# A mixture-of-experts stage with its down projection turned round and its combine weights spread by DMA

## The chip, the cores and the metric

One Trainium2 chip, one NeuronCore. The metric is the device time of one execution of the whole program in microseconds (us), lower is better. The core's engines run side by side, each through its own instruction list, and meet only at semaphores: TensorE (PE, with its weight loads as PEld), VectorE (DVE), ScalarE (ACT), GpSimd (POOL) and SyncE (SP), which here issues every DMA. A DMA moves data by up to 16 DMA engines.

## What is computed

A stack of four layers on 2 x 512 tokens of width 256: cross attention, a gated feed-forward, and so on. The change lies in one stage, the feed-forward of the second layer (`L1_ffn`), a mixture of 64 routed experts of hidden width 64, of which each token keeps 8, and 2 shared experts of hidden width 512:

```python
gates = softmax(x @ router_w + router_b)         # [T, 64]; the 8 largest are kept, divided by their sum
for e in range(64):                              # routed experts
    y += cw[:, e] * (silu(x @ w1[e] + b1[e]) @ w2[e] + b2[e])
for s in range(2):                               # shared experts, weight 1
    y += silu(x @ sw1[s] + sb1[s]) @ sw2[s] + sb2[s]
out = x_residual + y
```

(x is the normalised input; this is a shortening of the reference in plain words.) The kernel computes all 64 experts for all 1024 tokens; an expert that a token did not keep has combine weight `cw` 0.

## The kernel before

The program is a row of stages, each ended by a barrier of all engines. The stage here is `l1_experts_phase`. Its work is cut into N = 40 units of 128 hidden columns: 8 units of the shared experts (n = 0 to 7), then 32 units that each hold two routed experts (64 + 64 columns). T is 1024 tokens, P is 128, KC = 2 is the number of 128-chunks of the width 256, and Q = 2 halves of 512 tokens are called q.

The engines are software pipelined by hand. In period n, written by each engine's `period` function:

- TensorE computes the up projection of unit n into PSUM tile `up` (for each half q, six matmuls of 512 moving columns: weights `up_hi`/`up_lo` stationary, tokens `xnT_hi`/`xnT_lo` moving), for a routed unit one more matmul per half into `weight`, and then the down projection of unit n - 1 into PSUM tile `out`.
- ScalarE applies silu to `up` (L1617), splits the next unit's up weights into a high part (L1606, L1607), rounds `hidden` to its high part `h_hi` (L1625) and splits `dn_raw` (L1635).
- VectorE multiplies silu by the combine weights (L1682, `hidden`) and forms the low part `h_lo` (L1686). GpSimd forms the low parts of the weights (L1651, L1664).
- SyncE loads unit n's weights in two transfers, `load_up` (L1534, 128 partitions of 1028 bytes) and `load_dn` (L1537, 128 partitions of 1 KB), into raw buffers that there are two of (s = n % 2).

Every fp32 product is three matmuls of split operands, in `mm3` (L73 to L75): high by high, then the two mixed ones. In the down projection each matmul has 128 tokens of `h` stationary and 256 columns of `dn` moving, 8 token chunks by 3 matmuls = 24 per unit.

**The combine weights.** `l1_router` makes them as `exps` [128 tokens, 8 chunks, 64 experts] on VectorE during shared periods 0 to 3. A routed unit needs them with hidden columns on the partitions: partition j of unit n wants the 1024 weights of the expert that column j belongs to. Before, they are split into three bf16 parts (`split_parts`, after period 4), turned by TensorE (`turn_parts`, after period 5), copied by ScalarE, and then each period's matmul with the 0/1 matrix `select` (L1571) writes each expert's row to 64 partitions of PSUM tile `weight`. A second turn (`turn_weights`, after period 6) makes `cwT` [64 experts, 1024 tokens] in fp32, with which `add_biases` (after period 7) adds the b2 terms.

At the end, in period 40, the last down projection ends bank by bank, and VectorE adds `out` to the residual `g.x` and takes statistics (L1692, L139). The next stage is `l2_project_phase`.

Two transfers of an earlier stage come into the prediction. `return_inverses` (L838) stores a 128-partition tile of 16 values per partition into `inverse_rows`, which has 4 partitions: 128 rows of 64 bytes. `load_max` (L620) stores `neg_rows`, 12 partitions of 512 bytes, into 3 partitions of `q_stack`. A third, `phi_a<-fside` (L1838), loads 128 rows of 4 KB into 128 partitions. `sums<-avs` (L832) writes 32 partitions.

Of the kernel before, what the change touches and what calls it, by code (L numbers as in the profile page):

```python
# [17 lines left out]
F32 = mybir.dt.float32  # L18
F32R = mybir.dt.float32r
BF16 = mybir.dt.bfloat16  # L20
# [1340 lines left out]
def l1_router(nc, ctx, g, d, banks):  # L1361
# [4 lines left out]
    HALF = E1 // 2  # L1366

# [7 lines left out]
    parts = sb("cw_parts", [P, TC, 2, 3, HALF], BF16)  # L1375
    r = Shared()
    r.cwT = sb("cwT", [P, T])
    r.cw_partsT = sb("cw_partsT", [3 * HALF, 2, T], BF16)
# [3 lines left out]
    parts_done, parts_turned, dve_steps = g.sem("cw_parts_done"), g.sem("cw_parts_turned"), g.sem("r1_dve_steps")  # L1382
    r.parts_copied, cw_turned, r.cw_copied = g.sem("cw_parts_copied"), g.sem("cw_turned_done"), g.sem("cw_copied")
# [15 lines left out]
    def turn_parts(pe):  # L1399
        pe.wait_ge(parts_done, 1)  # L1400
        pe.wait_ge(ready, 1)
        for h in range(2):
            for c in range(TC):
                last = pe.transpose(banks.bitcast(BF16)[0:3 * HALF, h, c * P:(c + 1) * P],
                                    parts[:, c, h, :, :].rearrange("p a e -> p (a e)"), g.ident16[:, :])
            last.then_inc(parts_turned, 1)
# [12 lines left out]
    def copy_parts(act):  # L1419
        for h in range(2):  # L1420
            act.wait_ge(parts_turned, h + 1)
            act.activation(r.cw_partsT[:, h, :], banks.bitcast(BF16)[0:3 * HALF, h, :], ACT.Copy).then_inc(r.parts_copied, 1)

    def copy_weights(act):
        act.wait_ge(cw_turned, 1)
        act.activation(r.cwT[0:E1, :], banks[0:E1, :, :], ACT.Copy).then_inc(r.cw_copied, 1)
# [22 lines left out]
    def keep_largest(dve):  # L1449
# [4 lines left out]
        divide(dve)  # L1454

    def split_parts(dve):
        halves = exps[:, :, :].rearrange("p c (h e) -> p c h e", h=2)
        rest = shifted[:, :, :].rearrange("p c (h e) -> p c h e", h=2)
        own.link(dve.tensor_copy(parts[:, :, :, 0, :], halves))
        own.link(dve.tensor_tensor(rest, halves, parts[:, :, :, 0, :], ALU.subtract))  # L1460
# [995 lines left out]
```

## Time and profile before

| what | value |
|---|---|
| median of 3 runs | 1619.1 us (1615.59 to 1621.07) |
| profiled execution, span from its first to its last instruction | 1613.2 us |
| what lies around the span (median less span) | 5.9 us |
| the stage here, from its first DMA issue to the next stage's | 883.4 to 1151.5 us of the span |
| mean granted TensorE clock | 0.952 of full |
| TensorE busy over the span | 93% |

The page of the profile has no time of its own for the profiled execution beside its span, so the span and the 5.9 us are what the sums are made against. Times inside the span are counted from its first instruction. A matmul's recorded duration is longer than the distance to the next one, since matmuls are pipelined; what a stream of them costs is read from start to start.

### The profile page before, as it was taken

Reading aid. Unit: us, or ns where it says so; the run is one execution under the profiler, and the core shown is the slowest. Engines: PE = TensorE matmul, PEld = TensorE weight load, DVE = VectorE, ACT = ScalarE, POOL = GpSimd, SP = SyncE. Lnnn points to the kernel's source line nnn. Section 1 sums busy time; section 2 is a strip of 40 time slices with the busy share of each in tenths; the row PEclk is TensorE's granted clock in tenths of the full one; section 3 lists DMA queues with packets and bytes.
Section 4 is the critical chain, followed back from the end, with each engine's and each line's share of the span. In section 5 each row is a group of like instructions: output and inputs, shape, how many; then the busy total and the mean of one; then the engine's idle time right before and its main releaser. Section 6 shows DMA issues by size and latency. Waiting matters only on the chain. (4 is left out here: it accounts for less than half of the span.)

```text
span 1613.2 us, 26635 instructions
## 1 busy us (share of the span) xinstructions
PE 1503.4 (93%) x9326; PEld 1222.4 (76%) x9326; DVE 923.3 (57%) x1698; ACT 705.9 (44%) x1102; POOL 286.0 (18%) x317
## 2 busy tenths in 40 slices
PE   5899999899999999999996999999789799998894
PEld 4444444688888888888886888888677688887884
DVE  6788886545455554555558534444556445556555
ACT  5266666244343443434332555555333434343431
POOL 2111100022122221212210222222010112220110
PEclk8899999799999999999998899999899899999996
DMA  6711210111111111111100111111011211101000
GB/s 232 221 31 32 60 30 3 53 40 39 59 39 59 39 50 47 39 59 39 59 7 29 47 40 39 46 39 46 23 53 52 73 39 39 59 26 40 0 0 27
DMA packets 44836, 78.78 MB, mean 49 GB/s; under 512 B 7567, under 2 KB 27541, under 8 KB 43893
## 3 DMA queue, kind: packets, MB, share of 16 engines
q1 hardware_dynamic: 44789, 78.14, 15.8%
q8 instruction: 31, 0.51, 0.1%
q14 instruction: 16, 0.13, 0.0%
HBM read 67.40 MB, written 10.49 MB: 48 GB/s over the span
## 5 line engine op out<-in xcount | busy, mean ns | idle before, releaser
L1238 DVE TENSOR_TENSOR hidden_l<-silu_l,up_l 128x512 f32<-128x512 f32 x176 | 121.0, 688 | 305.7 <-ACT silu_l L1178 305.7
L73 PE MATMUL out_l<-dn_hi_l,h_hi_l 128*128 128x256 f32 x1024 | 295.4, 288 | 0.7 <-POOL dn_lo_l L1664 0.7
L1178 ACT ACTIVATE silu_l<-gate_l 128x512 f32<-128x512 f32 x176 | 105.2, 598 | 425.2 <-PE up_l L75 425.2
L75 PE MATMUL out_l<-dn_hi_l,h_lo_l 128*128 128x256 f32 x1024 | 289.5, 283 | 0.0
L74 PE MATMUL out_l<-dn_lo_l,h_hi_l 128*128 128x256 f32 x1024 | 289.4, 283 | 0.0
L73 PEld LDWEIGHTS out_l<-dn_hi_l,h_hi_l 128*128 128x128 f32 x1024 | 196.4, 192 | 2.8 <-issue 0.8
L74 PEld LDWEIGHTS out_l<-dn_lo_l,h_hi_l 128*128 128x128 f32 x1024 | 196.0, 191 | 2.8
L75 PEld LDWEIGHTS out_l<-dn_hi_l,h_lo_l 128*128 128x128 f32 x1024 | 196.0, 191 | 0.0
L798 DVE TENSOR_REDUCE maxima<-a_scores 128x1 f32<-128x512 f32 x256 | 164.6, 685 | 40.3 <-PE a_scores L736 39.1
L1210 POOL TENSOR_TENSOR gu_lo_l<-gu_raw_l,gu_hi_l 128x1024 fp32r<-128x1024 f32 x42 | 100.7, 2398 | 407.7 <-ACT gu_hi_l L1170 407.7
L1262 DVE SCALAR_TENSOR_TENSOR x_sb<-out_l,cw,x_sb 128x256 f32<-128x256 f32 x352 | 150.0, 477 | 30.6 <-PE out_l L75 24.9
L765 ACT ACTIVATE probs<-b_scores 128x1024 f32<-128x1024 f32 x128 | 131.0, 1023 | 66.6 <-PE b_scores L695 64.5
L73 PE MATMUL gate_l<-xnT_hi_n,gu_hi_l 128*128 128x512 f32 x352 | 139.7, 397 | 4.3 <-DVE xnT_lo_n L191 4.3
L1244 DVE TENSOR_TENSOR h_lo_l<-hidden_l,h_hi_l 128x512 fp32r<-128x512 f32 x176 | 139.3, 791 | 4.4
L74 PE MATMUL gate_l<-xnT_lo_n,gu_hi_l 128*128 128x512 f32 x352 | 139.3, 396 | 0.0
L75 PE MATMUL gate_l<-xnT_hi_n,gu_lo_l 128*128 128x512 f32 x352 | 138.9, 395 | 0.0
L73 PE MATMUL up_l<-xnT_hi_n,gu_hi_l 128*128 128x512 f32 x352 | 138.4, 393 | 0.0
L75 PE MATMUL up_l<-xnT_hi_n,gu_lo_l 128*128 128x512 f32 x352 | 138.0, 392 | 0.0
L74 PE MATMUL up_l<-xnT_lo_n,gu_hi_l 128*128 128x512 f32 x352 | 138.0, 392 | 0.0
L1183 ACT ACTIVATE h_hi_l<-hidden_l 128x512 fp32r<-128x512 f32 x176 | 110.3, 627 | 10.3 <-DVE hidden_l L1238 10.3
L1682 DVE TENSOR_TENSOR hidden_l<-silu_l,weight_l 128x512 f32<-128x512 f32 x64 | 44.0, 687 | 111.7 <-ACT silu_l L1617 111.7
L1617 ACT ACTIVATE silu_l<-up_l,b_l 128x512 f32<-128x512 f32 x80 | 55.1, 689 | 108.1 <-PE weight_l L1571 88.9
(369 smaller groups left out, 2835.4 us busy)
## 6 DMA issues: line engine op xcount, KB each, us to landing
gu_raw_l<-w_units SPq DMA_DIRECT2D x44, 512.0 KB, 3.8
dn_raw_l<-w_units SPq DMA_DIRECT2D x44, 256.0 KB, 2.7
k_stack<-k_stacks SPq DMA_DIRECT2D x8, 768.0 KB, 5.7
up_raw_l<-w SPq DMA_DIRECT2D x40, 128.5 KB, 2.1
dn_raw_l<-w SPq DMA_DIRECT2D x40, 128.0 KB, 2.1
phi_a<-fside SPq DMA_DIRECT2D x8, 512.0 KB, 3.3
k_stacks<-kq_parts SPq DMA_DIRECT2D x8, 384.0 KB, 2.6
q_stack<-q_stacks SPq DMA_DIRECT2D x8, 384.0 KB, 6.4
```

The costliest lines, as they stand in the source:

```text
L73: pe.matmul(out, lhs[0], rhs[0], start=start, stop=False, skip_group_check=True)
L74: pe.matmul(out, lhs[0], rhs[1], start=False, stop=False, skip_group_check=True)
L75: return pe.matmul(out, lhs[1], rhs[0], start=False, stop=stop, skip_group_check=True)
L765: act.activation(probs[u % 4][:, :, :], b_scores[:, u % 2, :, :], ACT.Exp, scale=SCALE).then_inc(exp_done, 1)
L798: dve.tensor_reduce(maxima[k // 16][:, i // 2, i % 2:i % 2 + 1], a_scores[:, k % 2, :], X, ALU.max).then_inc(a_read, 1)
L1178: act.activation(silu[:, q % 2, :], gate[:, q % 2, :], ACT.Silu).then_inc(silu_done, 1)
L1183: act.activation(h_hi[s][:, fc, half * 512:(half + 1) * 512], hidden[:, q % 2, :], ACT.Copy).then_inc(h_hi_done, 1)
L1210: pool.tensor_tensor(gu_lo[s][:, :, :, :], gu_raw[s][:, :, :, :], f32(gu_hi[s][:, :, :, :]), ALU.subtract).then_inc(gu_lo_done, 1)
L1238: dve.tensor_tensor(hidden[:, q % 2, :], silu[:, q % 2, :], up[:, q % 2, :], ALU.mult).then_inc(hidden_done, 1)
L1244: dve.tensor_tensor(h_lo[s][:, fc, t], hidden[:, q % 2, :], f32(h_hi[s][:, fc, t]), ALU.subtract).then_inc(h_lo_done, 1)
L1262: last = dve.scalar_tensor_tensor(g.x[:, c, :], out[:, b, j, :], weight, g.x[:, c, :], ALU.mult, ALU.add)
L1617: act.activation(silu[:, q, :], up[:, q, :], ACT.Silu, bias=b1[s][:, :]).then_inc(silu_done, 1)
```

## The change

1. **Down projection turned round.** The down weights become stationary and 512 tokens move: for each half of the tokens and each 128-chunk of the width one `mm3`, 4 x 3 = 12 matmuls of 512 columns per unit. `out` now holds the transposed output. `add_biases` is turned likewise. At the end ScalarE copies `out` to the new SBUF tile `outT`, TensorE turns it back in 16 transposes into the PSUM tile `front` (which `up` is now a part of), and VectorE adds that to the residual.
2. **Combine weights spread by DMA.** The matrix `select`, its matmul in each routed period, and the split, turn and copy of bf16 parts are gone. `turn_weights` runs after period 5 rather than 6. `cwT` is stored to DRAM as `cw_rows` [64, 1024]; for each routed unit `load_spread` reads its two rows of 4 KB, each 64 times over, into the 128 partitions of `spread[s]` (two buffers). VectorE waits for it before the unit's multiplications. The experts of a unit are now 2m and 2m + 1.

```diff
@@ l1_router @@
     def turn_weights(pe):
+        pe.wait_ge(kept, 1)
         for c in range(TC):
-            if c % 4 == 0:
-                pe.wait_ge(r.parts_copied, c // 4 + 1)
             last = pe.transpose(banks[0:E1, c // 4, c % 4 * P:(c % 4 + 1) * P], exps[:, c, :], g.ident[:, :])
...
@@ block.sync @@
-                sp.dma_start(select[:, :, :], d["select"]).then_inc(b2_loaded, 16)
-                with sp.Fori(0, (N - 2) // 2) as i:
+                def load_spread(m, pair, s):
+
+                    rows = g.cw_rows[bass.ds(2 * pair, 2), :].rearrange("e (o t) -> e o t", o=1).to_broadcast([2, H1, T])
+                    sp.dma_start(spread[s][:, :], rows).then_inc(spread_loaded[s], 16)
+
+                def load_unit(m, s):
+
+                    sp.wait_ge(up_lo_done, m - 1)
+                    load_up(m, s)
+                    sp.wait_ge(dn_lo_done, m - 1)
+                    load_dn(m, s)
+
+                for m in range(2, NS):
+                    load_unit(m, m % 2)
+                sp.wait_ge(router.cw_copied, 1)
+                sp.dma_start(g.cw_rows[:, :], router.cwT[0:E1, :]).then_inc(rows_stored, 16)
+                sp.wait_ge(rows_stored, 16)
+                for m in (NS, NS + 1):
+                    load_spread(m, m - NS, m % 2)
+                    load_unit(m, m % 2)
+                with sp.Fori(0, (N - NS - 2) // 2) as i:
                     for s in range(2):
-                        sp.wait_ge(up_lo_done, 2 * i + s + 1)
-                        load_up(2 * i + s + 2, s)
-                        sp.wait_ge(dn_lo_done, 2 * i + s + 1)
-                        load_dn(2 * i + s + 2, s)
+                        m = NS + 2 + 2 * i + s
+                        load_unit(m, s)
+                        sp.wait_ge(hidden_done, Q * (m - 1))
+                        load_spread(m, 2 + 2 * i + s, s)
@@ block.tensor, period @@
-                            if pair is not None:
-                                pe.wait_ge(hidden_done, Q * n + q - 1)
-                                last = pe.matmul(weight[:, q, :], select[:, bass.ds(pair, 1), :].rearrange("p o m -> p (o m)"),
-                                                 router.cw_partsT[:, s, t], start=True, stop=True)
...
-                        for c in range(TC):
-                            t = slice(c * P, (c + 1) * P)
-                            last = mm3(pe, out[:, c // 2, c % 2, :], (h_hi[o][:, t], h_lo[o][:, t]),
-                                       (dn_hi[o][:, :], dn_lo[o][:, :]), isinstance(n, int) and n == 1 and c % 2 == 0, not has_up)
+                        for h in range(2):
+                            t = slice(h * 512, (h + 1) * 512)
+                            for dc in range(KC):
+                                f = slice(dc * P, (dc + 1) * P)
+                                last = mm3(pe, out[:, h, dc, :], (dn_hi[o][:, f], dn_lo[o][:, f]),
+                                           (h_hi[o][:, t], h_lo[o][:, t]), isinstance(n, int) and n == 1, not has_up)
...
+                def return_output(pe):
+
+                    for h in range(2):
+                        pe.wait_ge(outT_done, KC * (h + 1))
+                        for c in range(4):
+                            for dc in range(KC):
+                                last = pe.transpose(front[:, 2 * h + c // 2, c % 2 * D + dc * P:c % 2 * D + (dc + 1) * P],
+                                                    outT[:, h, dc, c * P:(c + 1) * P], g.ident[:, :])
+                            if c % 2 == 1:
+                                last.then_inc(returned, 1)
@@ block.scalar @@
+                def copy_output(act):
+                    for h in range(2):
+                        for dc in range(KC):
+                            act.wait_ge(bank_done, KC * h + dc + 1)
+                            act.activation(outT[:, h, dc, :], out[:, h, dc, :], ACT.Copy).then_inc(outT_done, 1)
@@ block.vector, period @@
+                        dve.wait_ge(spread_loaded[s], 16 * (uses - NS // 2))
...
-                            dve.tensor_tensor(hidden[:, q, :], silu[:, q, :], weight[:, q, :], ALU.mult).then_inc(hidden_done, 1)
+                            dve.tensor_tensor(hidden[:, q, :], silu[:, q, :], spread[s][:, q * 512:(q + 1) * 512], ALU.mult).then_inc(hidden_done, 1)
@@ four_layers @@
+        g.cw_rows = nc.dram_tensor("cw_rows", [E1, T], F32, kind="Internal").ap()
```

**Where instructions move.** First SyncE's queue in the experts' stage. Before, the loop over the units holds two loads per unit:

```order
L1546 ISA
L1534 ISA
L1534 DMA up_raw_l<-w 128x257
L1537 ISA
L1537 DMA dn_raw_l<-w 128x256
L1534 ISA
```

(ISA rows are waits and register work.) In the changed program, at the same place, the store of `cw_rows` and the first spread stand ahead of unit 8's loads:

```order
L1516 DMA dn_raw_l<-w 128x256
L1540 DMA cw_rows<-cwT 64x1024
L1528 DMA spread_l<-cw_rows 128x1x1024
L1513 DMA up_raw_l<-w 128x257
L1516 DMA dn_raw_l<-w 128x256
L1528 DMA spread_l<-cw_rows 128x1x1024
```

So unit 8's up weights are now queued behind a store, a wait for its landing, and a spread; and in the loop that follows, each unit's two loads are followed by its spread on the same queue.

Second, TensorE's queue in a routed period. Before, from the end of the up projection's second half into the down projection:

```order
L75 MATMUL up_l<-xnT_hi_n,up_lo_l 128x512
L1571 MATMUL weight_l<-cw_partsT,select_l 128x512
L73 MATMUL out_l<-dn_hi_l,h_hi_l 128x256
L74 MATMUL out_l<-dn_lo_l,h_hi_l 128x256
L75 MATMUL out_l<-dn_hi_l,h_lo_l 128x256
```

and the same place of the changed program:

```order
L75 MATMUL front_l<-xnT_hi_n,up_lo_l 128x512
L73 MATMUL out_l<-h_hi_l,dn_hi_l 128x512
L74 MATMUL out_l<-h_lo_l,dn_hi_l 128x512
L75 MATMUL out_l<-h_hi_l,dn_lo_l 128x512
```

The matmul with `select` has gone, and the three-matmul group of 256 columns, which stood 8 times, is one of 512 columns, which stands 4 times.

## Rows read from the trace of the kernel before

**Rows 1.** The page, part 1: busy time and share of the span by engine.

```profile
PE 1503.4 (93%) x9326; PEld 1222.4 (76%) x9326; DVE 923.3 (57%) x1698; ACT 705.9 (44%) x1102; POOL 286.0 (18%) x317
```

**Rows 2.** Busy time by stretch: shared periods, routed periods; clock, DMA share, GB/s last.

```profile
core 0: us, PE busy (x) PEld busy (x) DVE busy (x) ACT busy (x) POOL busy (x), PEclk, DMA share, GB/s
...
889.43:946.21 56.78, 56.52 (x353) 51.09 (x353) 23.03 (x56) 32.69 (x65) 13.62 (x16) 0.94 0.15 39
946.21:1143.25 197.04, 196.41 (x1218) 165.43 (x1217) 85.42 (x128) 103.00 (x222) 51.57 (x63) 1.00 0.15 39
```

**Rows 3.** The timeline, TensorE in one routed period: start, duration, instruction.

```profile
1001.55 0.39 PE L73 MATMUL up_l<-xnT_hi_n,up_hi_l 128*128 128x512 f32 x1
...
1002.71 0.39 PE L75 MATMUL up_l<-xnT_hi_n,up_lo_l 128*128 128x512 f32 x1
...
1004.93 0.28 PE L74 MATMUL out_l<-dn_lo_l,h_hi_l 128*128 128x256 f32 x1
...
1007.20 0.28 PE L75 MATMUL out_l<-dn_hi_l,h_lo_l 128*128 128x256 f32 x1
```

**Rows 4.** The select matmul: all 64, with first and last start (us).

```profile
L1571 PE MATMUL weight_l<-cw_partsT,select_l x64: 391/392/392, 947.8 to 1139.4; 96*128 96x512 bf16 x64
```

**Rows 5.** The longest waits in the routed periods: in total, times, longest.

```profile
DVE hidden_l L1682 <- ACT silu_l L1617: 103.2, 61, 2.6
```

**Rows 6.** The timeline from the end of period 5 to the first routed period.

```profile
929.31 1.05 PE L1404 MATMUL weight_l<-ident_sb,cw_parts 128*96 128x128 bf16 x16
...
935.92 1.03 PE L1412 MATMUL weight_l<-ident_sb,exps 128*64 128x128 f32 x8
...
941.72 1.00 ACT L1426 ACTIVATE cwT<-weight_l 64x1024 f32<-64x1024 f32 x1
...
942.87 3.69 PE L1594 MATMUL out_l<-b_l,cwT 66*128 66x256 f32 x16 [0.26 <-ACT cwT L1426]
```

**Rows 7.** DMA issues of the whole trace: count, KB each, median us to landing.

```profile
dn_raw_l<-w SPq DMA_DIRECT2D x40, 128.0 KB, 2.1
phi_a<-fside SPq DMA_DIRECT2D x8, 512.0 KB, 3.3
...
out<-x_sb SPq DMA_DIRECT2D x4, 256.0 KB, 2.0
```

**Rows 8.** DMA from 286 to 288 us, where inverse_rows is written.

```profile
DMA packets 132, 0.01 MB, mean 4 GB/s; under 512 B 132, under 2 KB 132, under 8 KB 132
...
inverse_rows<-sums SPq DMA_DIRECT2D x1, 8.0 KB
```

**Rows 9.** DMA from 259.5 to 261.2 us, where neg_rows goes to q_stack.

```profile
q1 hardware_dynamic: 15, 0.01, 1.3%
...
q_stack<-neg_rows SPq DMA_DIRECT2D x1, 6.0 KB
```

**Rows 10.** DMA from 1200 to 1206 us, one load of phi_a, in 40 slices.

```profile
DMA  0000000000000939358989998300000000000000
GB/s 0 0 0 0 0 0 0 0 0 0 0 0 0 164 82 218 82 246 328 382 328 410 437 410 328 137 0 0 0 0 0 0 0 0 0 0 0 0 0 0
...
q1 hardware_dynamic: 144, 0.52, 26.7%
```

**Rows 11.** That load alone by stretch: us, clock, share of 16 DMA engines, GB/s.

```profile
1202.04:1203.90 1.86, 1.00 0.87 286
```

**Rows 12.** The timeline of the last unit, from its first weighted product on.

```profile
1138.88 0.69 DVE L1682 TENSOR_TENSOR hidden_l<-silu_l,weight_l 128x512 f32<-128x512 f32 x1 [2.40 <-ACT silu_l L1617]
...
1143.28 0.35 PE L73 MATMUL out_l<-dn_hi_l,h_hi_l 128*128 128x256 f32 x1 [0.66 <-POOL dn_lo_l L1664]
...
1149.11 0.75 DVE L139 BATCH_NORM_STATS2 stats_sb<-x_sb 128x6 f32<-128x256 f32 x2
```

**Rows 13.** The timeline, TensorE in the next stage, just after it stood idle.

```profile
1157.89 0.63 PE L75 MATMUL acc_p<-ctxT_hi_sb,wqkv_lo_p 128*128 128x512 f32 x1
...
1158.32 0.63 PE L73 MATMUL acc_p<-ctxT_hi_sb,wqkv_hi_p 128*128 128x512 f32 x1
```

More of the change, by code:

```diff
@@ L1492, in l1_experts_phase @@
         b2 = sb("b2", [E1 + ES1, D])
-        select = sb("select", [3 * E1 // 2, PAIRS1 // 2, P], BF16)
-        up = ctx.enter_context(nc.psum_tensor("up_l1", [P, 2, 512], F32))
-        weight = ctx.enter_context(nc.psum_tensor("weight_l1", [P, 2, 512], F32))
-        out = ctx.enter_context(nc.psum_tensor("out_l1", [P, TC // 2, 2, D], F32))
+        spread = two("spread", [P, T])
+        outT = sb("outT", [P, 2, KC, 512])
+        front = ctx.enter_context(nc.psum_tensor("front_l1", [P, 4, 512], F32))
+        up, routing = front[:, 0:2, :], front[:, 2:4, :]
+        out = ctx.enter_context(nc.psum_tensor("out_l1", [P, 2, KC, 512], F32))
         def sem(name):
@@ L1579, in period @@
                         pe.wait_ge(h_lo_done, Q * n)
-                        for c in range(TC):
-                            t = slice(c * P, (c + 1) * P)
-                            last = mm3(pe, out[:, c // 2, c % 2, :], (h_hi[o][:, t], h_lo[o][:, t]),
-                                       (dn_hi[o][:, :], dn_lo[o][:, :]), isinstance(n, int) and n == 1 and c % 2 == 0, not has_up)
-                            if not has_up and c % 2 == 1:
-                                last.then_inc(bank_done, 1)
+                        for h in range(2):
[4 more added lines that the diff above has]
+                                           (h_hi[o][:, t], h_lo[o][:, t]), isinstance(n, int) and n == 1, not has_up)
+                                if not has_up:
+                                    last.then_inc(bank_done, 1)
                         if has_up:
@@ L1589, in add_biases @@
                 def add_biases(pe):
[L1591 removed]
+                    pe.wait_ge(b2_loaded, 16)
                     pe.wait_ge(router.cw_copied, 1)
[L1593 to L1595 removed]
+                    for h in range(2):
+                        for dc in range(KC):
+                            pe.matmul(out[:, h, dc, :], b2[:, dc * P:(dc + 1) * P], router.cwT[0:E1 + ES1, h * 512:(h + 1) * 512],
+                                      start=False, stop=False, skip_group_check=True)
+                def return_output(pe):
[7 more added lines that the diff above has]
+                                last.then_inc(returned, 1)
                 pe.sem_inc(down_free, 2)
@@ L1599, in _ @@
                 norm.on_tensor(pe)
-                periods(pe, period, {0: router.take_logits, 5: router.turn_parts, 6: router.turn_weights, 7: add_biases})
+                periods(pe, period, {0: router.take_logits, 5: router.turn_weights, 7: add_biases})
+                return_output(pe)
             @block.scalar
@@ L1644, in _ @@
                 norm.high(act, 1)
-                periods(act, period, {1: router.exponentials, 5: router.copy_parts, NS - 1: last_copies})
+                periods(act, period, {1: router.exponentials, 5: router.copy_weights, NS - 1: last_shared})
+                copy_output(act)
             @block.gpsimd
@@ L1672, in _, with period @@
             def _(dve):
-                def period(n, s, uses, next_uses, pair):
+                def period(n, s, uses, next_uses):
                     if uses is None:
@@ L2410, in _arrange @@
         if n >= len(shared):
-            pair, half = divmod(n - len(shared), 2)
-            e = half * (E1 // 2) + 2 * pair
+            e = 2 * (n - len(shared))
             up = np.concatenate([i["L1_ffn_w1"][e], i["L1_ffn_w1"][e + 1]], axis=1)
```

82 lines of the change are left out of this document (29 added, 53 removed).

## The prediction

> **What bounds the kernel now.** I read the page's busy times first: TensorE is busy 93% of the span, no other engine over 57% [rows 1]. Then the windows of this stage: TensorE works 56.5 of 56.8 us in the shared periods and 196.4 of 197.0 us in the routed ones, at full clock there, while the DMA engines are 15% busy [rows 2]. The waits of the routed periods hold no DMA: VectorE waits for ScalarE, which follows TensorE [rows 5]. So here time is TensorE's instruction stream. From start to start, a 512-column matmul costs (1002.71 - 1001.55) / 5 = 0.232 us and a 256-column one (1007.20 - 1004.93) / 19 = 0.1195 us [rows 3]. The period follows from both: 14 x 0.232 + 24 x 0.1195 = 6.12 us, and the select matmuls say the same, 191.6 us from first to last less 1.6 inside a period, over 31 periods = 6.13 us [rows 4].
>
> **The change on TensorE.** A routed period becomes 12 + 12 matmuls of 512 columns: 24 x 0.232 = 5.57 us, 0.56 less. Nearly all of that is the two select matmuls; the turned projection itself gives 24 x 0.1195 - 12 x 0.232 = 0.08 us. The first turn of 16 small transposes (1.05 us, [rows 6]) goes too, the biases stay the same number of columns. If TensorE stayed the bound, this would be worth some 19 us. Whether it does hangs on the new transfer.
>
> **How long a spread takes.** It moves 128 rows of 4 KB, 512 KB, as much as one load of phi_a, which lands in 3.3 us [rows 7]. But the source is written as 2 rows, each read 64 times, and the trace shows that a transfer's outermost count matters. Packets beyond the data rows are completions, one from each DMA engine used: phi_a, 128 rows outermost on both sides, has 144 = 128 + 16 [rows 10]. inverse_rows, 128 rows at the source and 4 outermost at the destination, has 132 = 128 + 4 [rows 8]. neg_rows, 12 at the source and 3 at the destination, has 15 = 12 + 3 [rows 9]. In all three the number of engines is the largest up to 16 that divides both outermost counts. For 2 and 128 that is 2. I take two engines, each with 64 rows of 4 KB.
>
> The Trainium skill has this as a rule, in DMA: Bandwidth & Descriptors, "Why a DMA increments its semaphore by 16 and not by 1": the engines used are the largest number up to 16 that divides both patterns' slowest dimension other than 1, and its rules for kernel authors warn of just such a leading small count. The three rows above agree; by it too the spread has 2 engines, and the sum below is unchanged.
>
> A 4 KB row on one engine: phi_a's best slice is 437 GB/s on 16 engines = 27.3 GB/s each, 0.150 us a row; the mean of its last seven full slices is 375 GB/s, 0.175 us [rows 10]; over the whole load, 286 GB/s on 87% of 16 engines is 20.5 GB/s each, 0.20 us [rows 11], and simply 1.86 us for 8 rows is 0.23, start-up and all. A spread pays the start-up once in 64 rows, and 14 engines do not compete with it, so I take 0.16, near the best slice, and keep 0.150 and 0.23. 64 x 0.16 = 10.2 us. The same two engines also carry 16 of the rows of about 1 KB of each unit's up and down weights: 39 GB/s at a share of 0.15 of 16 engines is 16 GB/s each, 0.06 us a row [rows 2], 1.0 us. **So the two engines are taken for 11.2 us per unit, twice TensorE's 5.57.**
>
> **Does the queue keep them busy?** Two spread buffers are there. Spread m + 2 is issued once VectorE has multiplied unit m and GpSimd has ended its dn_lo, for which I estimate 5 us after spread m has landed, from the tail [rows 12]: first product at 1138.88, last unit's dn_lo released at 1143.28, 4.4. Some 1 us later it reaches the engines. That is well within the 11.2 us that spread m + 1 takes, so the engines run without a gap. VectorE now waits in every routed period; behind it stand h_lo and with it the down projection, and ScalarE's h_hi. The next unit's up weights stand behind the spread on the same two engines, so ScalarE's split and TensorE's up projection start late as well, but they land just behind it and add nothing to the period.
>
> TensorE will stand idle about half of each period, and where it did so before, 512 columns cost 1158.32 - 1157.89 = 0.43 us [rows 13], the lower of its two clocks. Even then 24 x 0.43 = 10.3 us fit into 11.2. I cost that at nothing in the loop; it would be bound only if the spread took under 9.
>
> **The sum.** Positions in the span. Period 5 of TensorE ends at 929.31 [rows 6], less 5 x 0.08: 928.9. The turn of the weights 1.03 and the copy 1.00 [rows 6] give 930.9. The store, 256 KB, is like that of out, 2.0 to landing [rows 7], plus 0.4 to issue: 933.3. A transfer's fixed part is 2.1 for a load of 8 small rows per engine [rows 7] less 8 x 0.06 = 1.6; the first spread lands at 933.3 + 1.6 + 10.2 = 945.1, the second 11.2 later, 956.3. The first weighted product of unit 9 waits for it. Thirty more units at 11.2: 956.3 + 336 = 1292.3 for unit 39. Before, this product began at 1138.88 [rows 12]. **+153.4 us.**
>
> The tail before: 10.98 us from there to the end of the last statistics at 1149.86 [rows 12]. After: the second product no longer waits for its silu, so the down projection starts at +3.5 instead of +4.4; 12 matmuls at 0.43 = 5.1; the last copy 0.7; the last 8 transposes, 1.03 at full clock [rows 6], 1.7 estimated at the lower; add and statistics 1.4: 12.6. **+1.7 us** (with the full clock +0.6).
>
> Total +155.1 us: on the span 1613.2 + 155.1 = 1768.3, and with 5.9 around it, which is on the median 1619.1 + 155.1 = **1774 us**.
>
> **The rivals.**
>
> *The change does what it says (16 engines).* Then a spread lands in about the 3.3 us of phi_a, is issued a period ahead and stays hidden while it lands within some 6.5 us; TensorE remains the bound. 32 x 0.56 + 7 x 0.08 + 1.05 = 19.5 saved, 0.6 lost in the tail: 1600 us. For it: the copies are equal in size to those that keep up now. Against it: rows 8 and 9, both of them transfers whose two sides differ in shape as this one's do. It decides from somewhere between 4 and 8 engines: with 4 a unit takes them 32 x 0.16 + 1.0 = 6.1 us, as much as a period now; with 8, 3.6, under TensorE's 5.57. Chance 0.07. The Trainium skill's fit for a transfer (the same page, "Anatomy of one DMA", 2.0 us + bytes / 436 GB/s) gives 3.2 us for 512 KB and would lead here; it has no term for the number of engines.
>
> *Two engines, dearer rows.* Reading one 4 KB row over and over, or gaps between transfers, could make a row cost phi_a's 0.20 to 0.23 us. Each 0.01 is 0.64 us a unit, on 32 spreads 20 us: 1856 to 1917 us. For it: phi_a over its whole length; against it, that start-up is most of the difference. Chance 0.12.
>
> *TensorE's lower clock decides.* If, at 0.43 us a matmul, up and down projection also had to wait on one another's results, TensorE's 10.3 us plus about 1.8 for splitting late weights would make 12.1 a period: 0.9 x 30 = 27 on top, 1801 us. Against it: those 1.8 us overlap the down projection of the unit before. Chance 0.08, inside my range.
>
> *The forecast itself*, two engines at 0.150 to 0.175 us a row: 0.73.
>
> **How the numbers follow.** At 0.150 a row the sum falls by 0.64 x 32 = 20 us, and if the small rows cost 0.05, by 5 more: 1749; at 0.175 it rises by 31: 1805. The range takes these, the clock rival, and a little of the dearer rows: 1747 to 1835 us, which leaves out the 16-engine case and most of the dearer one. About 0.3% (5 us) is what a measurement of this kernel can tell from no change. Faster by more: 0.07 (the first rival). Within it: 0.01, since only about 4 engines would land there. Slower: 0.92.
>
> **What would show it.** Right: of each spread, 128 packets and 2 completions; 11 us from product to product of successive units; VectorE waiting for spread_l in some 31 periods, 5 us each or more; DMA share near 2/16 of the engines plus the weights' part, at some 70 GB/s; a granted clock below 1 in the routed periods. Step by step on TensorE: 0.232 us from one turned down matmul to the next wherever the clock is full. Wrong: if the spread lands in under 6 us, the change is a gain of some 19 us and my whole sum falls; if periods are 11 us but VectorE waits for ScalarE, the late weights decide and not the spread.

## The result and the profile after

| | before | changed |
|---|---|---|
| median, range, runs | 1617.7 us (1615.6 to 1621.1, 4) | 1777.9 us (1777.4 to 1778.4, 4) |
| span of the profiled execution | 1613.2 us | 1776.4 us |
| mean granted clock | 0.952 | 0.914 |

The ratio is 1.098 (95% interval 1.0965 to 1.1002): the changed kernel is 160 us slower. The forecast was 1774 us, the range 1747 to 1835.

The page of the changed kernel: part 1; then from part 5 the group of the weighted products with the idle time before it; then from part 6 the transfers (KB each, us to landing).

```profile
PE 1553.1 (87%) x8774; PEld 1237.4 (70%) x8774; DVE 922.5 (52%) x1694; ACT 706.6 (40%) x1104; POOL 286.1 (16%) x317
...
L1699 DVE TENSOR_TENSOR hidden_l<-silu_l,spread_l 128x512 f32<-128x512 f32 x64 | 45.8, 717 | 258.3 <-DMA spread_l<-cw_rows 230.6
...
spread_l<-cw_rows SPq DMA_DIRECT2D x32, 512.0 KB
...
up_raw_l<-w SPq DMA_DIRECT2D x40, 128.5 KB, 16.3
dn_raw_l<-w SPq DMA_DIRECT2D x40, 128.0 KB, 7.4
```

VectorE stood 230.6 us before its 64 products for the spread, where no wait on a DMA was before [rows 5]. The down weights, 2.1 us to landing in [rows 7], now take 7.4, and the up weights, issued behind a spread, 16.3: two of the engines that carry them have a spread to move as well. (In e7 below, with no spread in the loop, both land in 2.1 us.) The page gives no landing for the spreads; it is read from the product that waits.

The windows over the routed periods, as [rows 2]: us, busy time and count of each engine, clock, DMA share, GB/s.

```profile
core 0: us, PE busy (x) PEld busy (x) DVE busy (x) ACT busy (x) POOL busy (x), PEclk, DMA share, GB/s
950.00:1300.00 350.00, 238.52 (x768) 181.31 (x768) 86.82 (x128) 104.00 (x226) 52.24 (x64) 0.80 0.20 69
```

768 matmuls, 24 for each of 32 units, take TensorE 238.5 of 350 us even at a mean clock of 0.80. At a share of 0.20 of 16 engines, 3.2 engines are busy on the mean; as e8 shows below, the spreads alone keep nearly two busy, and the weight loads are the rest. 69 GB/s is what the forecast named (some 70).

The waits from 956 to 1290 us: engine, line, releaser, us in total, times, longest.

```profile
POOL up_lo_l L1667 <- ACT up_hi_l L1617: 236.5, 31, 8.9
DVE hidden_l L1699 <- DMA spread_l<-cw_rows: 223.6, 29, 8.9
ACT b_l L1616 <- DMA up_raw_l<-w: 186.0, 30, 7.1
```

The loads and spreads from 990 to 1100 us, with the number of packets:

```profile
DMA packets 4184, 7.89 MB, mean 72 GB/s; under 512 B 340, under 2 KB 2900, under 8 KB 4184
...
spread_l<-cw_rows SPq DMA_DIRECT2D x10, 512.0 KB
up_raw_l<-w SPq DMA_DIRECT2D x10, 128.5 KB, 16.4
dn_raw_l<-w SPq DMA_DIRECT2D x10, 128.0 KB, 7.6
```

The count of small packets shows the engines: 20 weight loads with 16 completions each are 320, and 10 spreads add the 20 that are left of 340, **two completions per spread, so two engines each**.

VectorE's timeline, the first product of unit 10, of unit 38 and of unit 39:

```profile
978.73 0.69 DVE L1699 TENSOR_TENSOR hidden_l<-silu_l,spread_l 128x512 f32<-128x512 f32 x1 [8.85 <-DMA spread_l<-cw_rows]
...
1288.36 0.69 DVE L1699 TENSOR_TENSOR hidden_l<-silu_l,spread_l 128x512 f32<-128x512 f32 x1 [7.26 <-DMA spread_l<-cw_rows]
...
1299.08 1.29 DVE L1699 TENSOR_TENSOR hidden_l<-silu_l,spread_l 128x512 f32<-128x512 f32 x2 [7.05 <-DMA spread_l<-cw_rows]
```

(1299.08 - 978.73) / 29 = **11.05 us from unit to unit**, where 11.2 was forecast. The stage's first load is issued at 886.11 us here and at 883.37 before; from it to the end of the last statistics are 428.3 us, before 266.5: 161.8 more.

The start is where the trace differs from the forecast most. SyncE's timeline: the spreads of units 8 and 9, unit 9's up weights, and what follows.

```profile
936.71 0.65 SPq L1528 DMA_DIRECT2D spread_l<-cw_rows  x1
...
938.92 0.56 SPq L1528 DMA_DIRECT2D spread_l<-cw_rows  x1
939.53 3.14 SPq L1513 DMA_DIRECT2D up_raw_l<-w  x1
953.80 0.33 SPq L1516 DMA_DIRECT2D dn_raw_l<-w  x1
...
965.09 0.33 SPq L1516 DMA_DIRECT2D dn_raw_l<-w  x1
965.76 0.57 SPq L1528 DMA_DIRECT2D spread_l<-cw_rows  x1
```

The load at 953.80 is unit 9's down weights, that at 965.09 unit 10's, and 965.76 is the spread of unit 10. ScalarE stood still meanwhile for the up weights of unit 8, then of unit 9:

```profile
950.26 0.20 ACT L1616 ACTIVATE b_l<-up_raw_l 128x1 f32<-128x1 f32 x1 [10.04 <-DMA up_raw_l<-w]
...
961.08 0.20 ACT L1616 ACTIVATE b_l<-up_raw_l 128x1 f32<-128x1 f32 x1 [5.51 <-DMA up_raw_l<-w]
```

The DMA engines from 956.5 to 967 us in 40 slices:

```profile
DMA  0110110110111111000000000000000200005770
GB/s 31 62 62 31 62 62 31 62 62 31 62 62 47 39 43 47 31 23 4 0 0 0 0 0 0 0 0 0 0 0 0 62 0 0 0 0 39 179 273 8
```

After about 961.3 almost nothing moves until a load's burst at 966.

The tail: TensorE's last down projection and the turn back, then VectorE's additions and statistics.

```profile
1302.49 0.76 PE L73 MATMUL out_l<-h_hi_l,dn_hi_l 128*128 128x512 f32 x1 [4.33 <-POOL dn_lo_l L1680]
...
1307.32 0.63 PE L75 MATMUL out_l<-h_hi_l,dn_lo_l 128*128 128x512 f32 x1
1307.75 2.37 PE L1601 MATMUL front_l<-ident_sb,outT_l 128*128 128x128 f32 x16
```

```profile
1308.84 0.69 DVE L1709 TENSOR_TENSOR x_sb<-x_sb,front_l 128x512 f32<-128x512 f32 x1 [7.03 <-PE front_l L1601]
...
1313.69 0.75 DVE L139 BATCH_NORM_STATS2 stats_sb<-x_sb 128x6 f32<-128x256 f32 x2
```

### The profile page after: what moved, and what is told of

Read it like the earlier page. It is cut to its first block and busy times, and to the rows that moved or that the text cites. A ratio compares the mean times of both kernels' runs of the same rounds, so it can differ in the third digit from the quotient of the medians.

```text
span 1776.4 us, 25608 instructions
## 1 busy us (share of the span) xinstructions
PE 1553.1 (87%) x8774; PEld 1237.4 (70%) x8774; DVE 922.5 (52%) x1694; ACT 706.6 (40%) x1104; POOL 286.1 (16%) x317
## 5 line engine op out<-in xcount | busy, mean ns | idle before, releaser
L75 PE MATMUL out_l<-dn_hi_l,h_lo_l 128*128 128x256 f32 x704 | 199.2, 283 | 0.0
L74 PE MATMUL out_l<-dn_lo_l,h_hi_l 128*128 128x256 f32 x704 | 199.1, 283 | 0.0
L73 PE MATMUL out_l<-dn_hi_l,h_hi_l 128*128 128x256 f32 x704 | 199.0, 283 | 0.0
L73 PE MATMUL front_l<-xnT_hi_n,up_hi_l 128*128 128x512 f32 x160 | 89.1, 557 | 113.1 <-POOL up_lo_l L1667 105.1
L1699 DVE TENSOR_TENSOR hidden_l<-silu_l,spread_l 128x512 f32<-128x512 f32 x64 | 45.8, 717 | 258.3 <-DMA spread_l<-cw_rows 230.6
L73 PEld LDWEIGHTS front_l<-xnT_hi_n,up_hi_l 128*128 128x128 f32 x160 | 42.5, 265 | 136.3 <-ACT silu_l L1627 117.6
L74 PEld LDWEIGHTS out_l<-dn_lo_l,h_hi_l 128*128 128x128 f32 x704 | 134.9, 192 | 1.7
L73 PEld LDWEIGHTS out_l<-dn_hi_l,h_hi_l 128*128 128x128 f32 x704 | 134.9, 192 | 1.7
L75 PEld LDWEIGHTS out_l<-dn_hi_l,h_lo_l 128*128 128x128 f32 x704 | 134.9, 192 | 0.0
## 6 DMA issues: line engine op xcount, KB each, us to landing
up_raw_l<-w SPq DMA_DIRECT2D x40, 128.5 KB, 16.3
```

The costliest lines, as they stand in the source:

```text
L73: pe.matmul(out, lhs[0], rhs[0], start=start, stop=False, skip_group_check=True)
L74: pe.matmul(out, lhs[0], rhs[1], start=False, stop=False, skip_group_check=True)
L75: return pe.matmul(out, lhs[1], rhs[0], start=False, stop=stop, skip_group_check=True)
L1699: dve.tensor_tensor(hidden[:, q, :], silu[:, q, :], spread[s][:, q * 512:(q + 1) * 512], ALU.mult).then_inc(hidden_done, 1)
```

## Experiments

Each experiment's ratio is to executions of the kernel before that were timed with it; their median was 1618.6 us (e1, e2, e3, e6), 1619.1 (e4, e5, e8, e10) and 1619.6 (e7, e9, e11). In the edits, ... stands for lines left out.

### e1: the same copies as two transfers of one row each

```diff
-rows = g.cw_rows[bass.ds(2 * pair, 2), :].rearrange("e (o t) -> e o t", o=1).to_broadcast([2, H1, T])
-sp.dma_start(spread[s][:, :], rows).then_inc(spread_loaded[s], 16)
+for j in range(2):
+    row = g.cw_rows[bass.ds(2 * pair + j, 1), :].to_broadcast([H1, T])
+    sp.dma_start(spread[s][j * H1:(j + 1) * H1, :], row).then_inc(spread_loaded[s], 16)
...
-dve.wait_ge(spread_loaded[s], 16 * (uses - NS // 2))
+dve.wait_ge(spread_loaded[s], 32 * (uses - NS // 2))
```

> One edit to the changed kernel: each spread is issued as two transfers, one per expert, 64 copies of one row into 64 partitions, so that 64 stands outermost on both sides. Bytes, buffers and waits are the same. Theory (the number of DMA engines decides): each transfer uses 16 engines, 64 data packets and 16 completions each, a spread lands in some 3.5 us and is hidden; TensorE is the bound again at 5.57 us a unit, and the time is 1600 us (1596 to 1606). Rival (reading one row over and over is slow in itself, or the waits on the queue's order cost it): the time stays within 5% of 1778 us.

Measured: 1598.9 us (1598.4 to 1601.0, 4 runs), 0.988 of before [0.9856, 0.9906]. The same bytes come from the same rows, with the outermost count 64 on both sides. Its DMA from 990 to 1100 us, then two first products:

```profile
DMA packets 8884, 15.49 MB, mean 141 GB/s; under 512 B 1267, under 2 KB 6387, under 8 KB 8884
...
q1 hardware_dynamic: 8884, 15.49, 54.3%
...
spread_l<-cw_rows SPq DMA_DIRECT2D x40, 256.0 KB, 3.9
...
up_raw_l<-w SPq DMA_DIRECT2D x19, 128.5 KB, 3.3
```

```profile
949.39 0.69 DVE L1700 TENSOR_TENSOR hidden_l<-silu_l,spread_l 128x512 f32<-128x512 f32 x1 [4.67 <-ACT silu_l L1628]
...
1121.84 0.69 DVE L1700 TENSOR_TENSOR hidden_l<-silu_l,spread_l 128x512 f32<-128x512 f32 x1 [2.13 <-ACT silu_l L1628]
```

39 loads and 40 spreads at 16 completions each are 1264 of the 1267 small packets: 16 engines. Each half lands in 3.9 us, VectorE waits for ScalarE's silu, not for a DMA, and a unit takes (1121.84 - 949.39) / 31 = 5.563 us. The forecast's 5.57 for TensorE alone holds: from 950 to 1120 us TensorE is busy the whole time, at full clock. So the 160 us do not come from the 512 KB as such, nor from reading one row 64 times. The edit changes two things, the number of engines and the number of transfers; e6 and e10 below keep the two transfers and set the engines to four.

### e2: rows of half the length, on two engines still

```diff
-rows = g.cw_rows[bass.ds(2 * pair, 2), :].rearrange("e (o t) -> e o t", o=1).to_broadcast([2, H1, T])
+rows = g.cw_rows[bass.ds(2 * pair, 2), 0:T // 2].rearrange("e (o t) -> e o t", o=1).to_broadcast([2, H1, T // 2])
...
-dve.tensor_tensor(hidden[:, q, :], silu[:, q, :], spread[s][:, q * 512:(q + 1) * 512], ALU.mult).then_inc(hidden_done, 1)
+dve.tensor_tensor(hidden[:, q, :], silu[:, q, :], spread[s][:, :], ALU.mult).then_inc(hidden_done, 1)
```

> The changed kernel with half of each row: 2 KB rows of the first 512 tokens' weights, still 2 rows read 64 times outermost, used for both halves (the weights of the second half of the tokens are therefore those of the first). Theory (time of two engines, by bytes): 64 rows of 2 KB cost 5.0 to 5.4 us and the unit's own weights 0.9, so 6.0 to 6.4 us a unit in place of 11.05: 1612 to 1632 us. Rival (each descriptor or each repeated read costs a fixed time): about 11 us a unit stay, 1750 us or more.

Measured: 1622.1 us (1 run), inside the expectation. From 960 to 1130 us VectorE still waits for the spread:

```profile
DVE hidden_l L1699 <- DMA spread_l<-cw_rows: 82.9, 27, 4.7
```

First products at 963.49 (unit 10) and 1145.89 (unit 39) make 6.29 us a unit. Half the bytes in as many rows brought a unit from 11.05 to 6.29, 4.8 us less, so a row's price goes nearly with its bytes. With the forecast's estimate of 1.0 us for the small rows it is (11.05 - 1.0) / 64 = 0.157 us for 4 KB and (6.29 - 1.0) / 64 = 0.083 us for 2 KB. The packet records from 990 to 1100 us agree: in the middle (median) a packet took 0.159 us in the changed kernel and 0.084 us here.

### e3: the traffic without the wait

```diff
+scratch = two("scratch", [P, T])
...
-load_spread(m, 2 + 2 * i + s, s)
+sp.wait_ge(scratch_loaded[s], 16 * (i + 1))
+load_scratch(m, 2 + 2 * i + s, s)      # same rows, same queue, unread buffers
...
-dve.wait_ge(spread_loaded[s], 16 * (uses - NS // 2))
+dve.wait_ge(spread_loaded[s], 16)
```

> The changed kernel with the same spreads on the same queue at the same place, but from unit 10 on into two other buffers that no engine reads; VectorE multiplies by the first two units' weights throughout (so the combine weights of the other units are wrong). Theory (the two engines are the bound, since every unit's up and down weights stand behind the spread on them): still about 11 us a unit, 1765 to 1780 us, with ScalarE waiting for up_raw instead of VectorE for spread. Rival (the price is VectorE's wait, and a spread that nobody waits for costs nothing): 1600 to 1615 us.

Measured: 1771.8 us (1 run). No compute engine waits for the spreads of the loop any more, and the time stays. From 960 to 1130 us the waits are VectorE's for ScalarE and ScalarE's for the up weights:

```profile
DVE hidden_l L1711 <- ACT silu_l L1639: 126.6, 32, 7.5
...
ACT b_l L1628 <- DMA up_raw_l<-w: 92.8, 15, 7.2
```

SyncE does wait until the last spread into the same scratch buffer has landed, but that wait shows no time: it issues the spreads at 1006.79 and 1017.68, 0.76 and 0.68 us after the down load before them, and in the changed kernel that distance is 0.65 and 0.62. So VectorE's wait is where the slowness shows in the changed kernel, not its cause. The two engines carry spreads and a part of every weight load, and each unit needs one of both.

### e8: the spreads on a queue of their own

```diff
-sp.dma_start(spread[s][:, :], rows).then_inc(spread_loaded[s], 16)
+act.dma_start(spread[s][:, :], rows).then_inc(spread_loaded[s], 16)     # after dn_hi of unit n, for unit n + 2
...
```

The store of cw_rows moves to ScalarE's queue too.

> The store of the combine rows and all spreads are issued from ScalarE's queue (a DMA queue of its own), the weight loads stay on SyncE's; the spread is still one transfer that two DMA engines carry. Theory (two engines' time for 128 rows of 4 KB is the bound): the routed unit stays at 10.5 to 11.2 us, the whole at 1760 to 1785 us. Rival (the bound is the order in one queue: weights wait behind the spread, the spread behind SyncE's wait for the weights' splits): the unit falls under 8 us and the whole under 1700 us.

Measured: 1767.2 us (1766.6 to 1767.9, 2 runs), as the theory has it. From 990 to 1100 us, the new queue (packets, MB, share of 16 engines) and the up weights (KB, us to landing):

```profile
q10 hardware_dynamic: 1308, 5.28, 12.0%
...
up_raw_l<-w SPq DMA_DIRECT2D x10, 128.5 KB, 6.8
```

The up weights land in 6.8 us rather than 16.4, and that gives nearly nothing: first products at 952.05 (unit 8) and 1288.98 (unit 39) make 10.87 us a unit. A second queue does not bring a third engine. It does let one see the spreads by themselves: ten of them with 128 rows and 2 completions each are 1300 of the queue's 1308 packets, and 12.0% of 16 engines is 1.92 engines. **The spreads alone fill 1.92 of their two engines.**

### e5: the weights of units 8 and 9 ahead of their spreads

```diff
 for m in (NS, NS + 1):
-    load_spread(m, m - NS, m % 2)
     load_unit(m, m % 2)
+    load_spread(m, m - NS, m % 2)
```

> The spreads stay as they are (one transfer, two DMA engines); only for units 8 and 9 the two weight loads are issued ahead of the unit's spread. Theory (the stage is bound by the two DMA engines that carry the spreads, and in the changed kernel they stood idle once, from about 958 to 967 us, because unit 9's up weights were queued behind the spread of unit 9): that gap goes, spread 10 lands about 11 us sooner, each later unit still takes 11.0 us, about 1767 us in all. Rival 1 (the order at the start is hidden, the loop's pace alone decides): within 2 us of 1777.9. Rival 2 (the weights' place in the queue also makes the loop slow): well under 1760.

Measured: 1771.4 us (1769.0 to 1774.0, 4 runs), 6.5 less; no figure of the three expected. VectorE's first products of units 8, 9 and 10:

```profile
949.80 0.69 DVE L1699 TENSOR_TENSOR hidden_l<-silu_l,spread_l 128x512 f32<-128x512 f32 x1 [8.68 <-DMA spread_l<-cw_rows]
...
960.61 0.69 DVE L1699 TENSOR_TENSOR hidden_l<-silu_l,spread_l 128x512 f32<-128x512 f32 x1 [7.50 <-DMA spread_l<-cw_rows]
...
971.65 0.69 DVE L1699 TENSOR_TENSOR hidden_l<-silu_l,spread_l 128x512 f32<-128x512 f32 x1 [7.69 <-DMA spread_l<-cw_rows]
```

They are 10.8 and 11.0 us apart, so the hole is gone; but I had priced it at 11 us and it was some 6 (below), and the first spread now waits for the loads. Counted from the stage's first load (883.69 here, 886.11 in the changed kernel), that spread is issued 2.3 us later (52.85 against 50.60), unit 10's product comes 4.7 us sooner (87.96 against 92.62) and unit 39's 3.2 us sooner. The other half of the 6.5 us lies outside the stage, where executions differ by as much (last section).

### e6 and e10: four engines per spread

e6 writes the source of each of e1's two transfers with the outermost count 4:

```diff
-row = g.cw_rows[bass.ds(2 * pair + j, 1), :].to_broadcast([H1, T])
+row = g.cw_rows[bass.ds(2 * pair + j, 1), :].rearrange("e (o t) -> e o t", o=1).to_broadcast([4, H1 // 4, T])
```

> Two transfers per spread as in e1_two_dmas, but with the 64 copies written as 4 times 16, so that 4 stands outermost at the source. Theory (largest divisor of both outermost counts): each uses 4 engines, the same four, so 32 rows of 4 KB and 8 x 2 small ones per engine and unit: 5.1 + 0.9 = 6.0 us, just above TensorE's 5.57, time 1612 to 1625 us, 64 data packets and 4 completions per transfer. Rival (only the split of a transfer in two halves mattered): as e1_two_dmas, 1600 us.

Measured: 1653.9 us (1652.4 to 1661.4, 4 runs), 1.023 of before [1.0196, 1.0270], 29 us over the top of the expectation. Its DMA from 990 to 1100 us:

```profile
DMA packets 6316, 11.71 MB, mean 106 GB/s; under 512 B 595, under 2 KB 4414, under 8 KB 6316
```

The large packets are those of 30 weight loads and 30 transfers of the spreads. With 16 completions for each load and 4 for each transfer that makes 600 small ones, near the 595: four engines each. SyncE's and VectorE's timelines over two units:

```profile
993.64 1.33 SPq L1529 DMA_DIRECT2D spread_l<-cw_rows  x2
```

```profile
988.89 0.69 DVE L1700 TENSOR_TENSOR hidden_l<-silu_l,spread_l 128x512 f32<-128x512 f32 x1 [2.46 <-DMA spread_l<-cw_rows]
...
997.42 0.69 DVE L1700 TENSOR_TENSOR hidden_l<-silu_l,spread_l 128x512 f32<-128x512 f32 x1 [5.17 <-DMA spread_l<-cw_rows]
...
1003.17 0.69 DVE L1700 TENSOR_TENSOR hidden_l<-silu_l,spread_l 128x512 f32<-128x512 f32 x1 [2.49 <-DMA spread_l<-cw_rows]
```

The products do not come every 6 us but in pairs, 5.8 and 8.5 us apart; from unit 11 (973.39) to unit 39 (1178.11) it is 7.31 us a unit. A chain goes through each pair: the product at 988.89, the spread of the same buffer issued at 993.64, 4.75 us later, and its product at 1003.17, 9.53 after that. e10 shortens that chain, with the same four engines:

```diff
-load_unit(m, s)
+sp.wait_ge(up_lo_done, m - 1)
+load_up(m, s)
 sp.wait_ge(hidden_done, Q * (m - 1))
 load_spread(m, 2 + 2 * i + s, s)
+sp.wait_ge(dn_lo_done, m - 1)
+load_dn(m, s)
```

> The kernel with four DMA engines per spread (1653.9 us), with one edit: in the loop the spread of unit m + 2 is issued right after unit m's products, ahead of the wait for the low part of unit m's down weights, not behind it. Theory A (at four engines the round trip decides: a spread lands, the products, the splits, the issue 4.75 us after the landing, and 9.5 us until it has landed, 14.3 us for two units): the issue comes about 2 us sooner in each two units, so 16 round trips save about 30 us, 1620 to 1632 us. Theory B (the four engines' rate decides, with rows that take longer while more of them run): no gain, 1648 to 1656 us.

Measured: 1615.4 us (1612.9 to 1622.3, 10 runs), 0.998 of before [0.9964, 0.9990], 38.5 us less than e6 and a little more than expected. Product and next issue of that buffer:

```profile
990.64 0.69 DVE L1703 TENSOR_TENSOR hidden_l<-silu_l,spread_l 128x512 f32<-128x512 f32 x1 [2.03 <-DMA spread_l<-cw_rows]
...
1002.75 0.69 DVE L1703 TENSOR_TENSOR hidden_l<-silu_l,spread_l 128x512 f32<-128x512 f32 x1 [2.03 <-DMA spread_l<-cw_rows]
```

```profile
993.48 1.36 SPq L1529 DMA_DIRECT2D spread_l<-cw_rows  x2
```

It is 2.84 us from product to issue in place of 4.75, and 9.3 to the next product: 12.1 us for two units, over the loop (965.59 to 1146.44, units 10 to 39) 6.24 a unit, near the 6.1 of the engines. So at four engines the order in SyncE's queue is worth 1.07 us a unit. From the stage's first load to the end of the statistics the two traces differ by 33.4 us (305.8 against 272.4), and the medians by 38.5; the execution profiled here, at 1622.3 us, is the longest of the ten.

### e11: the same early spread with two engines

The edit of e10's loop, on e5.

> The kernel with two DMA engines per spread and the weights of units 8 and 9 ahead of their spreads (1771.4 us), with the edit that took the four-engine kernel from 1653.9 to 1615.4: in the loop the spread is issued ahead of the wait for the down weights' low part. Theory (with two engines the spread of one unit is under way the whole time in which the next one is waited for and issued, so the time between two units is the two engines' time): no gain, 10.8 to 11.1 us a unit, 1764 to 1772 us. Rival (the round trip from landing to issue is part of each unit here too): 2 to 3 us less for each two units, 1725 to 1745 us.

Measured: 1770.6 us (1769.4 to 1771.7, 2 runs), against 1771.4 for e5. First products of units 10 and 39 at 974.12 and 1291.74: 10.95 us a unit, against 11.10 in e5. The edit that was worth 38 us at four engines is worth 0.8 us in the medians and 0.15 us a unit (4 us) in the traces at two, where each spread is asked for long before its engines are free.

### e4: the turned projection alone

The kernel before, with the down projection, biases and tail of the changed one; select and its parts stay.

> The kernel before with the turned down projection alone; the select matmul and its split parts stay, nothing is spread by DMA. Theory (12 matmuls of 512 columns cost 0.08 us less per unit than 24 of 256, and the turn back at the end costs 2 to 3 us with the clock at full): -3.2 + 2.2, about 1 us less than before, ratio 0.998 to 1.001. Rival 1 (the turned projection is what makes the two-transfer kernel 1.2 per cent faster than before): ratio 0.990 or less. Rival 2 (its tail costs the 4.4 us that the changed kernel showed): ratio 1.001 to 1.003.

Measured: 1615.1 us (1612.3 to 1618.7, 11 runs), 0.997 of before [0.9956, 0.9981]: 4 us less in the medians, more than the 1 expected. Its first products of units 8 and 39:

```profile
951.07 0.69 DVE L1706 TENSOR_TENSOR hidden_l<-silu_l,front_l 128x512 f32<-128x512 f32 x1 [6.77 <-ACT silu_l L1634]
...
1137.52 0.69 DVE L1706 TENSOR_TENSOR hidden_l<-silu_l,front_l 128x512 f32<-128x512 f32 x1 [2.30 <-ACT silu_l L1634]
```

That is 6.015 us a unit; before it was 6.12 (from 949.12 to 1138.88). That is 0.11 rather than 0.08 less, 3.3 us over 31 periods, and the tail to the end of the statistics takes 13.5 us (1150.24 + 0.75 - 1137.52), 2.5 more than before. From the stage's first load (885.20) to the end of the statistics it is 265.8 us, 0.7 less than before, as the theory has it; where the other 3 us of the medians come from is open (below).

### e9: the first half turned back earlier

```diff
 for h in range(2):
     for dc in range(KC):
+        if not has_up and h == 1 and dc == 1:
+            return_half(0)
...
```

This is on e1.

> The two-transfer kernel (1598.9 us), with the transposes of the first half of the tokens placed ahead of the last group of three down matmuls instead of behind all of them. The copies of the first half end at about 0.2 us after the place where they are put, so TensorE loses some 0.2 us and VectorE's chain of four additions and statistics (5.6 us, one after the other) begins 0.6 us sooner. Theory: the first addition starts 7.0 us after the last unit's first product instead of 7.6, the stage ends 0.6 us sooner, 1598 us, not to be told from 1598.9 by the time. Rival (the additions could have started right with each finished bank): 3 us sooner, 1596 us.

Measured: 1598.6 us (1598.3 to 1600.9, 4 runs), the same as e1. In its trace the first addition starts at 1129.58, 7.12 us after the product at 1122.46; in e1 it is 7.60. So the theory holds, also in that the gain, 0.5 us of the stage (248.5 against 249.0), is too small for the medians: VectorE's four additions and eight statistics follow one another for 5.6 us, and this edit moves only their start.

### e7: no spreads after the first two

```diff
-sp.wait_ge(hidden_done, Q * (m - 1))
-load_spread(m, 2 + 2 * i + s, s)
-dve.wait_ge(spread_loaded[s], 16 * (uses - NS // 2))
+dve.wait_ge(spread_loaded[s], 16)
```

> The changed kernel with the first two spreads alone; later units read those two, so their weights are the wrong experts' (the same work on other numbers), and no spread is loaded in the loop. Theory (spreads that 16 engines carry are hidden, and all of the slowdown is the two engines' time): 5.56 us a unit as in the two-transfer kernel, 1596 to 1601 us. Rival (the 512 KB a unit cost the two-transfer kernel something as well, by late weights or contention): 5 us or more below 1598.9 us.

Measured: 1609.7 us (1606.8 to 1610.9, 4 runs), which neither theory gave: 11 us more than e1, which moves 16 MB more. I had forgotten that the first two spreads stay on two engines here. First products of units 11 and 39:

```profile
979.74 0.69 DVE L1697 TENSOR_TENSOR hidden_l<-silu_l,spread_l 128x512 f32<-128x512 f32 x1 [2.23 <-ACT silu_l L1625]
...
1135.51 0.69 DVE L1697 TENSOR_TENSOR hidden_l<-silu_l,spread_l 128x512 f32<-128x512 f32 x1 [2.13 <-ACT silu_l L1625]
```

From unit 11 on a unit takes (1135.51 - 979.74) / 28 = 5.563 us, e1's very figure, so in the loop the copies cost e1 nothing. Unit 11 itself comes 94.7 us after the stage's first load, and 80.0 after it in e1, 14.7 later: two slow spreads and the weights queued behind them cost that once. In the medians 11 of it is left; from the end of the stage to the end of the span this profiled execution takes 4.4 us less than that of e1 (last section).

## Why the prediction was right, and where it was off

**Two engines** (step "How long a spread takes"): right, by the completions (340 = 320 + 20, against 1264 in e1) and by the times: e1 with 16 engines takes 1598.9 us and e10, with as many transfers as e1 but four engines, 1615.4. The Trainium skill's rule (DMA: Bandwidth & Descriptors, "Why a DMA increments its semaphore by 16 and not by 1") gives 2, 4 and 16 engines for the changed kernel, e6 and e1, and the completions of each trace agree (340, 595 and 1267 small packets).

**0.16 us a row, 11.2 us a unit**: it took 11.05, and with the estimated 1.0 for the small rows 0.157 a row. From 990 to 1100 us the packet records have 0.159 us (median) and 0.164 (mean) for a 4 KB packet. The high end, 0.175 to 0.23, fell with it. The packets of the phi_a load in [rows 10] had the same median, 0.159, and a mean of 0.199: most of its rows were no dearer, and why some took longer is not shown.

**"The engines run without a gap"**: in the loop yes (1.92 of two engines filled in e8, and in e11 an earlier issue gains next to nothing), at the start no. Here the step failed. I costed the queue of units 8 and 9 as free. But unit 9's down load waits for GpSimd's dn_lo of unit 7, and GpSimd does the split of unit 8's up weights first; those stand behind spread 8, so ScalarE gets them at 950.26 and the load is issued at 953.80. A unit later the same ring closes again: unit 9's up weights stand behind spread 9 and reach ScalarE at 961.08, unit 10's down load is issued at 965.09, and spread 10 stands behind it, when the engines have been empty since 961.3. Unit 10's product was forecast 84.1 us after the stage's first load (956.3 + 11.2 - 883.4) and came 92.6 after it (978.73 - 886.11), 8.5 late: 0.7 in the issue of the first spread (50.6 for 49.9), about 1.5 in that spread (13.3 us from issue to product in e5, for 11.8), which leaves 6.3 for the hole. Twenty-nine units at 0.15 less gave 4.4 back: unit 39's product 413.0 us in, for 408.9.

**The tail, +1.7**: mis-sized. It took 1313.69 + 0.75 - 1299.08 = 15.4 us, not 12.6, so +4.4. The recorded terms, 3.5, 5.1, 0.7, 1.7 and 1.4, add up to 12.4 and not to 12.6. The +0.6 for the full clock does not follow from them either: with 12 matmuls at 0.232 and transposes of 1.03 they give 9.4, which is 1.6 less than before. The steps up to the transposes held (first matmul at +3.4, 0.43 us from one to the next), but all four additions wait for the turn back, which stands behind all twelve matmuls, and they take 5.6 us in a row; I had counted 1.4, that of the last alone. With the full clock (e1) the tail is 13.2 us, +2.2.

**The lower clock**: as forecast, the clock fell, to 0.80 on the mean in the routed periods. Not all 24 matmuls ran at the lower one, though: in the period at 1035 us most of the up projection came 0.43 us apart, after 3 us of idle time, and the down projection behind it 0.23 us apart. That the clock costs nothing in the loop was not tried by itself; it is argued from the 1.92 of two engines that the spreads fill in e8, at a pace of 10.87 us a unit. In e10 at four engines, with TensorE busy 102.8 of 110 us from 990 to 1100 us, the granted clock was 1.00.

**TensorE's part**: 5.57 forecast, 5.563 in e1. The turned projection gave 0.11 a unit in e4, not 0.08.

**The 5.9 us around the span**: wrong as a constant. In the changed kernel it is 2.0 (1778.4 for the profiled execution of span 1776.4), and it is 1.8 to 2.2 in every execution of the experiments. The profiled execution of before was then one of some 1615 us, 4 below the median that I added its difference to. That error and those above nearly cancel: the span was 8.1 us over the forecast, the median 3.9. Of the 8.1, 4.1 came up to unit 39 and 2.7 in the tail; 2.7 more is that the stage began later (886.11 for 883.37), and what follows the stage took 1.4 less.

**The rivals.** Sixteen engines: 1600 was its time, and e1, which makes its premise true, gave 1598.9. It was refuted for the change as written only. Its point of decision, however, is off: at four engines I put 6.1 us a unit and no change. e6 took 7.31 us a unit and 1.023 of the time before, since with two buffers the round trip decides there; with the order of e10 the estimate holds. Dearer rows and the clock: refuted by 11.05 a unit. The fit that the forecast put beside the sixteen engines, from the Trainium skill (DMA: Bandwidth & Descriptors, "Anatomy of one DMA"), is stated there for DMAs that GpSimd issues; SyncE issues those of this kernel.

## What to carry to other kernels

Before trusting a transfer's size, look at the outermost counts of both its sides and, in the trace, at its completions: of the same 512 KB, each half landed 3.9 us after its issue when all 16 engines carried it, and the whole took 11 us a unit as one transfer on two. Where DMA engines bind, taking a wait away moves it (e3) and another queue doesn't help (e8); where the round trip of a buffer binds, the place of the issue in the queue is worth much with no engine added (38.5 us from e6 to e10). And in a prologue follow each queue entry to what it waits for, since one order there can close a ring over three engines.

## What the runs showed of the hardware beyond the forecast

With four engines a spread was slower than its share in the presence of the other: 9.5 us from issue to product in e6, against the 5 or so of 32 rows at 0.157. Part of that is the spread before it and the weights. Rows also got dearer: in the packet records from 990 to 1100 us a 4 KB packet took 0.164 us on the mean in the changed kernel (two engines), 0.176 in e10 and 0.198 in e6 (four), and 0.236 in e1 (16). Why is not shown. Equal parts of the program also differ between executions: the stage's first load is issued at 883.4 to 886.7 us in the thirteen kernels, though nothing before it differs, and from the end of the stage to the end of the span it takes 459.5 us (e7) to 463.9 (e1). So of two profiled executions, differences under some 4 us are read inside the stage alone. That e4 gains some 4 us in the medians and 0.7 inside the stage, and e1 19.7 and 17.5 (266.5 - 249.0), is of that size, and its cause stays open.
